# Thirteen one-hots on VectorE and three on ScalarE in the first two batches of each gather, GpSimd's clears and copies behind them

## The reference, cut to what matters

```python
inds_sorted = _sorted_indices(coords)              # 4 orders of the 512 points of each batch
inds_list = [_window_inds(s) for s in inds_sorted] # 10 neighbours of each point in each order
g1 = _get_graph_features(f0, inds_list, perm1, W_lin1, b_lin1)      # gather, minus centre, attention
feats1 = lrelu(instance_norm(conv1(g1))).max(-1)
g2 = _get_graph_features(feats1, inds_list, perm2, W_lin2, b_lin2)  # the same on the new features
```

## Time and profile before

| | |
|---|---|
| median of three runs | 2161.54 us (2160.78 to 2163.72) |
| profiled execution, its own time | 2166.15 us |
| span of the profiled execution | 2164.4 us |
| gather of layer 1, first one-hot to last subtraction | 106.4 to 265.3 us |
| gather of layer 2, first one-hot to last subtraction | 670.6 to 828.4 us |
| PE, DVE, ACT, POOL busy over the span | 86%, 85%, 74%, 49% |

### The profile page before, as it was taken

One profiled execution on the slowest core, in us unless ns is written; L12 is line 12 of the kernel. 1 busy time (PEld: TensorE's weight loads), 2 busy tenths in 40 slices (PEclk: granted clock), 3 DMA queues, 4 the chain that ended last, 5 costly groups with the idle time before them and its releaser, 6 DMA issues. The chain is left out here.

```text
span 2164.4 us, 99543 instructions
## 1 busy us (share of the span) xinstructions
PE 1853.2 (86%) x37656; PEld 1269.9 (59%) x37656; DVE 1833.2 (85%) x3511; ACT 1592.1 (74%) x3296; POOL 1068.8 (49%) x1160
## 2 busy tenths in 40 slices
PE   4877589998976774999999994879999999999958
PEld 2333378888873333899999992424545545454522
DVE  8899889999996996898988986947888888878865
ACT  7899788888887995999999993575545555455532
POOL 1220089999990003788888880003445444544522
PEclk9976699999996667999999996999999999999978
DMA  1157866555642776454544431202222222222110
GB/s 37 34 120 173 188 149 133 128 130 129 130 94 71 176 175 156 101 111 105 109 107 107 108 79 56 86 29 89 78 83 87 73 87 86 74 87 83 58 57 20
DMA packets 434896, 215.53 MB, mean 100 GB/s; under 512 B 301195, under 2 KB 404267, under 8 KB 434680
## 3 DMA queue, kind: packets, MB, share of 16 engines
q1 hardware_dynamic: 431872, 212.24, 40.0%
q10 hardware_dynamic: 2936, 2.18, 0.4%
HBM read 161.35 MB, written 52.86 MB: 99 GB/s over the span
## 5 line engine op out<-in xcount | busy, mean ns | idle before, releaser
L1015 PE MATMUL pQ<-QM,QX 128*128 128x96 f16 x2880 | 299.5, 227 | 1.4 <-issue 1.4
L1013 PE MATMUL pQ<-neigh_lo,QX 128*128 128x64 f16 x2880 | 292.6, 195 | 3.1 <-issue 3.1
L1013 PEld LDWEIGHTS pQ<-neigh_lo,QX 128*128 128x128 f16 x2880 | 276.3, 103 | 3.5 <-issue 3.5
L2655 POOL TENSOR_TENSOR MT<-cb,decay 128x512 f32 (+1 forms) x128 | 175.1, 1389 | 206.5 <-DVE half L2566 151.6
L1015 PEld LDWEIGHTS pQ<-QM,QX 128*128 128x128 f16 x2880 | 274.7, 103 | 1.4 <-issue 1.4
L1570 PE MATMUL pQ<-QM,QX 128*128 128x64 f16 x2880 | 231.7, 206 | 0.0
L1568 PE MATMUL pQ<-neigh_lo,QX 128*128 128x32 f16 x2880 | 227.0, 182 | 0.0
L1568 PEld LDWEIGHTS pQ<-neigh_lo,QX 128*128 128x128 f16 x2880 | 218.4, 103 | 2.6
L1111 POOL TENSOR_TENSOR Dm<-Sc,mx 128x450 f32<-128x450 f32 x192 | 183.8, 957 | 70.3 <-DVE mx L1071 70.3
L1570 PEld LDWEIGHTS pQ<-QM,QX 128*128 128x128 f16 x2880 | 212.0, 104 | 0.1
L2623 DVE SCALAR_TENSOR_TENSOR cv_m<-pX,taps_m,cv_m 128x496 f32<-128x496 f32 (+2 forms) x192 | 137.6, 717 | 72.6 <-ACT cv_m L2529 55.9
(11 more groups left out here) (460 smaller groups left out, 5210.0 us busy)
## 6 DMA issues: line engine op xcount, KB each, us to landing
QM<-scratch_q SPq DMA_DIRECT2D x192, 240.0 KB, 2.6
QX<-scratch_q SPq DMA_DIRECT2D x768, 60.0 KB, 2.2
scratch_q<-QT SPq DMA_DIRECT2D x124, 360.0 KB, 5.1
Wo<-in_out_proj SPq DMA_DIRECT2D x64, 256.0 KB, 2.6
Wg<-in_in_proj SPq DMA_DIRECT2D x62, 256.0 KB, 2.6
Wh<-in_in_proj SPq DMA_DIRECT2D x62, 256.0 KB, 2.8
W_s<-in_in_proj SPq DMA_DIRECT2D x20, 256.0 KB, 2.6
CT<-scratch_c SPq DMA_DIRECT2D x192, 11.2 KB, 2.1
```

Of the source, the lines that this page charges most:

```text
L1013: nc.tensor.matmul(pQ[:, p, u // PB, o + 32:o + BW], qx[u], W["neigh_lo"][:, 0:O], start=False, stop=True, skip_group_check=True)
L1015: last = nc.tensor.matmul(pQ[:, p, u // PB, o:o + BW], qx[u], qm[u], start=False, stop=True, skip_group_check=True)
L2655: nc.gpsimd.tensor_tensor(MT[:, k1 % 2, h, :, :].rearrange("p q (b i) -> p q b i", b=4), P["cb"][:, bass.ds(r, 1), :, :].rearrange("p g q ...
```

## The change

In both gathers, for batches 0 and 1 alone (`lead`), DVE makes thirteen one-hots instead of ten (`HOT + MORE`) and ACT three instead of six. The three are counted on a semaphore of their own (`first_hot`), for which PE waits as well; ACT counts `late_hot` and `apart_ready` up by three itself, so that the later batches wait for the same numbers as before. ACT's order in batch 0 is one one-hot, `t16`, two one-hots; in batch 1 it is `t16` and three one-hots. DVE's `l16` of batch 0 stands behind all thirteen.

The two memsets of `QT` leave the group that the others wait for (`ZEROS = 4`). They now run when DVE has made the ten one-hots of batch 1, and SP waits for them (`turns_zeroed`) ahead of the first store of windows. ACT's wait for the strips of `cen` moves from its start to its first copy of `pcen`. In layer 1 POOL's clear of `CT` and of the first part of `QX` follow the memsets of `QT`, the other three of `QX` wait for the one-hots of batch 2, and the eight copies into `QM` for those of batch 3.

The part for layer 1; layer 2 has the same edits, without those to `CT`, `QX` and `QM`:

```diff
-        ZEROS = 6
+        MORE = 3
+        ZEROS = 4
...
+        def lead(b):
+
+            return isinstance(b, int) and b < 2
...
                     sp.wait_ge(q_v, b * QV + 5 * QV)
+                    if first(b):
+                        sp.wait_ge(turns_zeroed, 2)
                     for m in range(0 if isinstance(b, int) and b == B - 1 else M):
                         store_windows(sp, k3, r, m)
...
-            nc.gpsimd.memset(turns[:, :, :, PTS * K * RES:], 0.0).then_inc(pads_zeroed, 1)
-            nc.gpsimd.memset(turns[:, :, NSUB // RES:, 0:PTS * K * RES], 0.0).then_inc(pads_zeroed, 1)
             pool.wait_ge(pads_zeroed, ZEROS)
             for k in range(4):
                 pool.sem_inc(q_out[k], QO)
             pool.sem_inc(shifted, ND)
+            pool.wait_ge(hot_ready, 2 * HOT)
+            nc.gpsimd.memset(turns[:, :, :, PTS * K * RES:], 0.0).then_inc(turns_zeroed, 1)
+            nc.gpsimd.memset(turns[:, :, NSUB // RES:, 0:PTS * K * RES], 0.0).then_inc(turns_zeroed, 1)
             nc.gpsimd.memset(CT[:, :, :], 0.0).then_inc(ct_zeroed, 1)
             for k in range(0, NQ, 2):
+                if k == 2:
+                    pool.wait_ge(hot_ready, 3 * HOT)
                 nc.gpsimd.memset(QX[:, k:k + 2, :, :, :].rearrange("p k w h x -> p (k w h x)").bitcast(F32), 0.0)\
                     .then_inc(wide_zeroed, 1)
+            pool.wait_ge(hot_ready, 4 * HOT)
             for k in range(NQ):
                 for c in range(1, SEG):
                     nc.gpsimd.tensor_copy(wide(k, c), column(c)).then_inc(wide_ready, 1)
...
-                    for mt in range(HOT):
-                        if first(b) and mt == HOT // 2:
-                            dve.wait_ge(t16_ready, b + 1)
-                            v.tensor_tensor(l16[:, h, :], ptok[:, h, 0:NT * C], t16[:, h, :],
-                                            ALU.subtract).then_inc(l16_ready, 1)
+                    for mt in range(HOT + MORE if lead(b) else HOT):
                         v.tensor_scalar(onehot[:, h, mt, :], place[:, :],
                                         rank[:, bass.ds(b + perm[mt // NT] * B, 1), mt % NT], None,
-                                        ALU.is_equal).then_inc(hot_ready, 1)
+                                        ALU.is_equal).then_inc(hot_ready if mt < HOT else first_hot, 1)
+                    if first(b):
+                        dve.wait_ge(t16_ready, b + 1)
+                        v.tensor_tensor(l16[:, h, :], ptok[:, h, 0:NT * C], t16[:, h, :],
+                                        ALU.subtract).then_inc(l16_ready, 1)
...
                     pe.wait_ge(late_hot, b * LATE + LATE)
+                    if lead(b):
+                        pe.wait_ge(first_hot, b * MORE + MORE)
...
-            act.wait_ge(pads_zeroed, ZEROS)
             act.wait_ge(rank_turned, 2)
...
                     if first(b):
                         act.wait_ge(gathered, b + 1)
-                        hots(b, h, 0, 2)
+                        act.sem_inc(late_hot, MORE)
+                        act.sem_inc(apart_ready, MORE)
+                        distance(b, MORE)
+                        hots(b, h, MORE, MORE + 1)
...
-                    if not first(b):
+                    if lead(b) and not first(b):
+                        act.wait_ge(late_hot, b * LATE)
+                        act.sem_inc(late_hot, MORE)
+                        act.sem_inc(apart_ready, MORE)
+                        distance(b, MORE)
+                        hots(b, h, MORE, MORE + 1)
+                    elif not first(b):
                         act.wait_ge(late_hot, b * LATE)
                         hots(b, h, 0, 2)
...
-                    hots(b, h, 2, LATE)
+                    hots(b, h, MORE + 1 if lead(b) else 2, LATE)
...
+                    if first(b):
+                        act.wait_ge(pads_zeroed, ZEROS)
```

More of the change, by code:

```diff
@@ L647, in gather_windows @@
         late_hot = sem("late_hot")
+        first_hot = sem("first_hot")
+        turns_zeroed = sem("turns_zeroed")
         gathered = sem("gathered")
@@ L716, in _ @@
             turns = QT[:, :, :, :].rearrange("p k g x -> p k (g x)").rearrange("p k (w x) -> p k w x", x=32 * RES)
-            nc.gpsimd.memset(turns[:, :, :, PTS * K * RES:], 0.0).then_inc(zeroed, 1)
-            nc.gpsimd.memset(turns[:, :, NSUB // RES:, 0:PTS * K * RES], 0.0).then_inc(zeroed, 1)
             pool.wait_ge(zeroed, ZEROS)
```

7 lines of the change are left out of this document (6 added, 1 removed).

## The result

The changed kernel takes 2150.69 us, the median of five runs (2149.45 to 2153.05). The kernel before took 2162.30 us beside it (2160.78 to 2164.15). The ratio is 0.994 with an interval of 0.9929 to 0.9952, and the medians differ by 11.6 us. Forecast were 2149.8 us and a gain of 11.7.

A forecast was written before the change was run, and what follows sets the result against it. ACT's never-idle one-hot stream was taken to bound both gathers. Gains of 6.1 us in layer 1 and 5.6 in layer 2 sum to 11.7, taking the profiled 2166.15 to 2154.4, or 2149.8 us as median; range 2146.8 to 2154.0.

The forecast's parts named there:

- The bound: Both gathers: ACT's never-idle stream sets the end, so starting its steady part earlier at t16 of batch 2 gains 11.7 us.
- The first gather without a gap: Sign, both layers: the first gather follows PE's pcen of batch 1 directly, at 115.9 us in layer 1 and 678.63 in layer 2.
- `t16` of batch 2 at 12.3 and 12.9 us: Sign: this ACT copy comes that long after PE's first ptok began in layers 1 and 2, against 18.5 before.
- The rival of the earlier clock: Rival, chance 0.12: PE without gaps gets its faster clock earlier, shortening gathers and ptok by 1.3 us, to 2148.5 us.
- Three one-hots beside the first clear, up to 1.1 us late: Layer 1, batch 1: DVE's last three one-hots may each wait for a POOL memset, ending 1.1 us behind the first gather.
- Subtractions beside POOL: Layer 1: POOL's moved 15 us beside DVE's subtractions costs nothing; three subtractions still take 5.62 us.
- Its 4.3 us of spare time: Layer 1: DVE at 8.8 us a batch finishes its fifteenth subtraction at 249.0, against the last gather's end at 253.3.
- DVE's wait grows to 4 or 5 us: Sign: DVE's wait ahead of the last subtraction grows to that from 3.2 us.
- Later stages keep their length: Attention, Mamba and feed-forward only begin 11.7 us earlier and take as long as before.
- The sum: Both layers: 6.1 us in layer 1 plus 5.6 in layer 2 make 11.7 us.

The follow-up runs named there:

- after_lean: Changed kernel with four QM loads of layer 1 cut to 16 elements per partition and block; 2151.40 us, ratio 0.9937 to the kernel before.
- the two halves: Each part of the change alone on the kernel before: thirteen one-hots with POOL's work unmoved, 2153.72 us; POOL's work moved with ten one-hots, 2163.45 us.
- more2: Changed kernel with twelve one-hots on DVE and four on ACT in the first two batches; 2153.03 us, ratio 0.9941 to the kernel before.
- more4: Changed kernel with fourteen one-hots on DVE and two on ACT in the first two batches; 2150.50 us, ratio 0.9933 to the kernel before.
- lead1: Changed kernel with the thirteen/three split in batch 0 alone, batch 1 back at ten and six; 2156.17 us, ratio 0.9962 to the kernel before.
- turn_early: Changed kernel with PE's ptok of batch 2 ahead of the gather of batch 0 instead of behind it; 2153.84 us, ratio 0.9958 to the kernel before.
- lead3: Changed kernel with thirteen one-hots on DVE and three on ACT in batch 2 as well; 2151.93 us, run again 2154.86 us.
- lead3_lean: Changed kernel with thirteen/three in the first three batches and four QM loads of layer 1 cut to 16 elements per partition and block; 2152.63 us, ratio 0.9939.
- split_only: Kernel before with only the one-hots of batches 0 and 1 moved (thirteen DVE, three ACT), POOL's work left in place; 2153.72 us, ratio 0.9949.
- hot11: Changed kernel with eleven one-hots on DVE and five on ACT from batch 2 on; 2159.43 us, ratio 0.9972 to the kernel before.

## Why the prediction was right

*The bound.* Right. ACT's stream set the end of both gathers, and moving its `t16` of batch 2 moved the last subtraction by as much: 5.94 us at 121.23 against 127.17, and 5.79 at the end, in layer 1; 6.62 in layer 2, and 6.69 at the end, both counted from the first `ptok`. The experiments say it more strongly. In the nine kernels that leave ACT's work from batch 2 on as it was (before, after, `after_lean`, the two halves, `more2`, `more4`, `lead1`, `turn_early`), the last subtraction begins 132.2 to 132.5 us behind `t16` of batch 2, in both layers, while that copy itself comes anywhere from 11.8 to 18.5 us behind the first `ptok`.

*The first gather without a gap.* Right in both layers, at 115.33 and 672.84.

*`t16` of batch 2 at 12.3 and 12.9 us.* It came at 13.02 and 11.84. The mechanism held (ACT waits there, for `ptok`), and the term that was mis-sized is `ptok`: I gave layer 1 the 1.11 us that it had there and layer 2 its 1.91, and the changed kernel had them the other way round, 1.91 and 1.07. The errors, +0.7 and -1.1, nearly cancel, and that is luck: `lead3` and `lead3_lean` are the same up to the end of the gather, and this `ptok` of layer 1 took 1.07 us in one and 1.91 in the other. The rival of the earlier clock came true in layer 2, as the windows of after over the first gather and over the `ptok` behind it show:

```profile
672.84:676.50 3.66, 3.66 (x53) 1.50 (x56) 2.55 (x10) 3.59 (x8) 1.89 (x1) 0.50 0.07 20
676.90:677.90 1.00, 1.00 (x9) 1.00 (x10) 0.93 (x1) 0.00 (x1) 0.67 (x1) 1.00 0.22 61
```

The granted clock went from 0.50 to 1.00, that is from 1.2 to 2.4 GHz, at the end of a first gather ahead of which PE had run without a gap since 666.06; in the kernel before, with its gap of 1.59 us, that `ptok` took 1.91. The Trainium skill ("TensorE: Matmul & The Clock Gate", part 1), weighed in the prediction as speaking for this rival, agrees with layer 2. In layer 1 the rival did not come true: PE ran on from 108.21 without a gap too, and `ptok` of batch 2 still took 1.91 us, where it had taken 1.11 before the change. The last part has the clock there.

*Three one-hots beside the first clear, up to 1.1 us late.* It went the other way. DVE's thirteen took 3.71 us, no more than those of batch 0 with POOL idle (3.72), and POOL's clear was stretched to 2.02 us, and to 2.30 with fourteen one-hots in `more4`, from the 1.30 that it took in `lead1`, where the one-hots of batch 1 are over by then. POOL in `lead1` and `more4`:

```profile
118.11 1.30 POOL L1440 MEMSET QT<- 128x1440 f16 x1 [12.13 <-DVE onehot L1495]
...
116.81 2.30 POOL L1440 MEMSET QT<- 128x1440 f16 x1 [10.31 <-DVE onehot L1495]
```

With the clears first, in `split_only`, thirteen one-hots took 13.19 us. So here the side that had begun went first. The Trainium skill ("SBUF — State Buffer", section "Who interferes with whom") says of one instruction that whichever issues first keeps the shared ports for the whole of it. The trace agrees in who waited, and goes further: three or four one-hots in a row went ahead of the waiting clear, and not only the one that was running. I had cited the rule and then let each one-hot wait; DVE's row was the one that had begun.

*Subtractions beside POOL.* Right, and at the price of nothing that I had chosen between nothing and 15 us: 5.62 and 5.63 us for three beside memsets and copies. POOL's part got even faster: the three clears of `QX` took 4.96, 1.65 each, where four took 7.09, and the copies 4.29, where they took 4.81.

*DVE's wait grows to 4 or 5 us.* Wrong: 3.39 and 3.29. Its 4.3 us of spare time were counted from the first subtraction, with no other idle time. But DVE catches up with ACT before the last batch and stands idle for 0.33 to 0.37 us ahead of four remainders, 1.4 us in all in layer 1 (at 232.16 and at 241.38 for `t16`, for instance), so part of what it saves is spent by then. It changed nothing in the sum. As `lead3` and `hot11` suggest, it may matter for what comes next.

*Later stages keep their length.* Right for both attentions and Mamba, to within 0.5 us, as the table at the top shows. Wrong for the feed-forward in the profiled executions, by 3.9 us.

*The sum.* 11.7 us forecast, 11.6 between the medians, 12.5 in the gathers by the profiles. That the medians agree so closely is partly luck, since the five executions of either kernel lie some 3.5 us apart, the 48 of the kernel before beside the experiments went from 2159.49 to 2171.10, and the feed-forward alone can differ by 4 us between two executions, as the last part shows.

## What to carry to other kernels

Where two engines feed one gather, find the stream that never idles and ask only when its steady part begins: the end of the stage moved by what that instant moved, to 0.2 us, in two layers. Two edits that each bring a quarter can bring the whole together (1.5 and 1.5 us alone, 5.8 together, in layer 1), because each alone leaves the other engine late. And an engine's wait at the end of a stage should not be counted as free until it is known who uses that time: two kernels that spent DVE's wait found PE waiting for loads in the next stage, 2.8 to 6.9 us in all, where it had waited for at most 1.7, and were no faster than the change.

## What the runs showed of the hardware

The feed-forward, which no kernel here touches, took 73.4 to 74.1 us in eight of the fourteen profiled executions and 78.0 to 78.2 in six, and nothing in between. The windows over the feed-forward of before and then of after, columns as in the earlier trace rows:

```profile
2086.38:2164.40 78.02, 56.65 (x188) 18.05 (x188) 47.25 (x68) 25.11 (x36) 11.41 (x9) 0.76 0.12 46
```

```profile
2073.59:2147.70 74.11, 52.25 (x188) 17.48 (x188) 47.15 (x68) 25.11 (x36) 11.40 (x9) 0.82 0.13 48
```

DVE, ACT and POOL are busy for the same time in both (to 0.1 us), and PE for 4.4 us more in before, at a granted clock of 0.76 instead of 0.82. What differs is when the clock leaves its lower level, 1.2 GHz, for 2.4: by the clock records of the traces it is at the lower level when the stage begins, in all fourteen, and rises 16.3 us into it in after and 19.1 in before. All fourteen fall into line by this: 73.4 us where it rises at 12.0 or 12.1 (two), 74.0 to 74.1 where it rises at 16.2 or 16.3 (six), 78.0 to 78.2 where it rises at 19.0 to 19.5 (six). What sets that instant no run here shows. It isn't the instant at which the stage begins: `turn_early` began it at 2073.54 and took 78.06, after at 2073.59 and took 74.11. Nor is it clear that it hangs on the kernel: the three executions with three leading batches were all short and the two of `hot11` both long, but one profile of each is too little to say so. It is as large as most of what was tried here, and that is why the experiments above are read by stages. `split_only`, with 10.8 us gained over the whole and 6.3 in its gathers, and `turn_early`, with gathers like those of after and 2153.84 us, each fit better with it than without. So some of the 11.6 us of the change may be of this kind, and not the change's own.

The second surprise is a row that seems to disagree with itself. Over the `ptok` of batch 2 in layer 1 of after the granted clock reads 1.00:

```profile
119.30:121.20 1.90, 1.90 (x15) 1.90 (x10) 1.73 (x1) 0.00 (x0) 1.90 (x3) 1.00 0.14 36
```

and it reads 1.00 up to 130 us in all of that start, while `ptok` took 1.91 us, `pcen` 2.05 and the gather 4.03: lengths that in layer 2 went with 0.50. That 1.00 is not a reading. The first clock record in the trace of after begins at 127.2 us, and a stretch without a record counts as 1.00. The first record, of 1.00, begins at 122.3 in before, at 119.0 in `more4`, at 118.9 in `lead3` and at 127.1 in `lead3_lean`, and a `ptok` that runs just behind it is short. The next `ptok` in after, and `ptok` of batch 2 in `more4`, `lead3` and `lead3_lean`:

```profile
126.95 1.16 PE L1563 MATMUL ptok<-ident_g,small 32*128 32x32 f32 x8
...
119.00 1.07 PE L1563 MATMUL ptok<-ident_g,small 32*128 32x32 f32 x8
...
118.92 1.07 PE L1563 MATMUL ptok<-ident_g,small 32*128 32x32 f32 x8
...
118.81 1.91 PE L1563 MATMUL ptok<-ident_g,small 32*128 32x32 f32 x8
```

In all fourteen traces the `ptok` of batch 2 took 1.07 to 1.11 us where the first record had begun by its end, and 1.75 to 1.91 where it had not. So by the lengths the clock was at its lower level until then, and in layer 1 it rose later in after than in before. The 0.68 of the earlier trace rows holds some 16 us of such empty time, and is too high by that. At the start of a trace the lengths are to be trusted, and the granted clock only from its first record on.
